# Full node ids in the buckets, tiles that run over their end, and all four marks of a step on VectorE, in a graph kernel on one core

## The reference, cut to what matters

```python
# x (6250,128); src, edge node ids (206250,); edge_attr_128 (206250,128); src is not sorted
edge_aggr = jnp.zeros((n, 128)).at[src].add(edge_attr_128)       # a sum of feature rows per node
combined  = concatenate([x, edge_aggr, global_feat repeated], -1) @ W_c + b_c
h = softplus(combined @ W1 + b1)
h = softplus(h @ W2 + b2)
out = layernorm(x + h @ W3 + b3)
```

## Time and profile before

| | |
|---|---|
| median of 3 runs | 2171.48 us (2169.77 to 2183.89) |
| the profiled execution | 2166.25 us |
| its span in the trace | 2164.6 us |
| PE busy | 1999.3 us (92%) |
| DVE, POOL, ACT busy | 1534.2, 1163.2, 843.7 us |
| placement, first to last `rank` | 72.4 to 1623.4 us |
| summing, first tile load to first MLP matmul | 1642.2 to 2082.8 us |

### The profile page before, as it was taken

The page is one execution under the profiler, slowest core; times in us unless marked ns, Lnnn a source line. Parts: engine busy times, 40 slices in busy tenths (PEclk is TensorE's granted clock), DMA queues, the critical chain, the costliest instruction groups (busy, mean ns, idle before and its releaser), DMA issues.

```text
span 2164.6 us, 62457 instructions
## 1 busy us (share of the span) xinstructions
PE 1999.3 (92%) x15732; PEld 1762.3 (81%) x15732; DVE 1534.2 (71%) x5104; ACT 843.7 (39%) x2517; POOL 1163.2 (54%) x1351
## 2 busy tenths in 40 slices
PE   6408999999999999999999999999996999999975
PEld 3307888888888888888888888888886999999952
DVE  7505776777677777777776777777775888888857
ACT  0002222222222222222222222222224888888877
POOL 2205665665665566656655556565564555455424
PEclk9658999999999999999999999999997999999998
DMA  9975665666656566566665565665556999999932
GB/s 353 150 140 153 173 175 167 174 178 170 178 171 176 173 170 180 168 177 171 173 178 164 168 183 168 170 181 173 176 153 222 296 285 284 284 284 283 284 98 55
DMA packets 345473, 414.30 MB, mean 191 GB/s; under 512 B 28261, under 2 KB 249465, under 8 KB 344273
## 3 DMA queue, kind: packets, MB, share of 16 engines
q1 hardware_dynamic: 284579, 247.08, 39.4%
q0 software_dynamic: 53184, 163.38, 26.1%
q10 hardware_dynamic: 7689, 3.60, 0.8%
HBM read 233.69 MB, written 180.24 MB: 191 GB/s over the span
## 4 chain that ended last, share of the span: by engine, by line
PE 69%; POOLq 6%; issue 6%; POOL 6%; another core or an unknown queue 4%; ACT 3%; ACTq 2%; DMA 1%; DVE 1%; SPq 0%; DVEq 0%
PE ps L953 55%; PE ps L961 5%; POOL sums L454 5%; POOLq L449 4%; PE ps L1019 3%; PE ps L938 3%; PE ps L932 2%; ACTq L759 2%; PE ps L936 1%; POOLq L453 1%; ACT arena L827 1%; DMA buckets<-arena,index 1%; ACT arena L830 1%; ACT arena L828 1%
## 5 line engine op out<-in xcount | busy, mean ns | idle before, releaser
L953 PE MATMUL ps<-arena 128*120 128x129 f32 x9672 | 1286.8, 282 | 73.2 <-ACT arena L784 73.1
L429 POOL DMA_INDIRECT buckets<-arena,index x806 | 893.1, 1108 | 664.6 <-ACT arena L784 300.6
L953 PEld LDWEIGHTS ps<-arena 128*120 128x120 f32 x9672 | 1128.4, 184 | 99.1 <-issue 73.2
L784 ACT ACTIVATE arena<-ps 120x387 f32<-120x387 f32 x806 | 397.8, 494 | 1146.5 <-PE ps L953 734.2
L614 DVE TENSOR_SCALAR arena<-slot_no,slot_f 128x360 f32<-128x360 f16 x1612 | 586.2, 404 | 0.0
L1019 PE MATMUL ps<-mark,members 128*128 128x128 f32 x3648 | 426.3, 279 | 19.8 <-ACT mark L859 19.8
L1019 PEld LDWEIGHTS ps<-mark,members 128*128 128x128 f32 x3648 | 418.7, 193 | 27.3 <-issue 20.0
L682 DVE TENSOR_SCALAR mark<-node_no,members 128x128 f32<-128x128 f16 x1368 | 365.0, 328 | 71.8 <-DMA members<-buckets 46.1
L601 DVE TENSOR_TENSOR picked<-hotc,ps 128x392 f32<-128x392 f16 x202 | 113.5, 562 | 348.2 <-PE ps L938 344.0
L454 POOL TENSOR_TENSOR sums<-sums,staged 128x128 f32 x456 | 216.0, 474 | 227.0 <-ACT staged L847 206.3
L620 DVE TENSOR_SCALAR reach<-block_no,arena 50x120 bf16<-50x120 f16 x806 | 196.8, 244 | 0.0
(11 more groups left out here) (121 smaller groups left out, 578.8 us busy)
## 6 DMA issues: line engine op xcount, KB each, us to landing
members<-buckets SPq DMA_DIRECT2D x456, 258.0 KB, 3.4
arena<-in_feats SPq DMA_DIRECT2D x201, 512.0 KB
buckets<-arena,index POOLq DMA_INDIRECT x806
buckets<-sums SPq DMA_DIRECT2D x4, 3096.0 KB, 26.4
arena<-in_xT SPq DMA_DIRECT2D x12, 250.0 KB, 5.8
xn<-in_x ACTq DMA_DIRECT2D x1, 2800.0 KB
out_rows<-xn SPq DMA_DIRECT2D x12, 224.0 KB
buckets<-sums SPq DMA_DIRECT2D x1, 1032.0 KB, 39.1
```

The source lines that it names most:

```text
L429: pool.indirect_dma_start(units, bass.IndirectOffsetOnAxis(ap=index[0:SLOTS, s, b:b + 1], axis=0), rows[0:SLOTS, b, :], None).then_inc(sca ...
L784: act.activation(rows[0:SLOTS, b, :], ps[0:SLOTS, MOVED + b, 0:BLK], ACT.Copy).then_inc(rows_ready, 1)
L953: mm = pe.matmul(ps[0:SLOTS, MOVED + b, r * ROWF:(r + 1) * ROWF], perm[0:TP, b, t, r * SLOTS:(r + 1) * SLOTS], feat[0:TP, s, b * TPB + t, ...
```

## The change

- The rows in the scratch carry their full node id plus one (`local1` is made in one operation from `ids_i`), no longer the id within the bucket.
- Buckets follow each other without alignment. A tile starts at any row, and its last rows may belong to the next bucket: their ids match none of the tile's 128 nodes. So the 11 pieces behind each bucket and the 52 zero tiles go; four small gap writes and one tile of zeros stay. The number of steps stays 456.
- A table `tile_row` holds each tile's first row. SP reads it into a register before each load (`value_load`) and then waits for `summed`.
- A mark compares `node_no + first_node` with the row's id: one DVE operation with two scalars read per partition, one of them at a place that the step number gives. DVE makes all four; ACT's L853 and L859 go.
- `window`, `first_node` and `past` are evicted by ACT behind its set-up work, before its first `set_locals`; DVE makes `tile_row` after the first body of `place`.
- `reach`, `goto3`, `boff1_16` and `ident16` are used over all 128 partitions (the added ones hold zeros), so the matmuls of `goto` and the last four of `rank` contract over 128 rows.

A step has one more mark and one more register operation. The diff, cut to its core:

```diff
-    SURE = -(-(E + K * STREAMS * GAP) // TROWS)
-    ZTILES = 12
+    ENDROW = E + K * STREAMS * GAP
...
@@ sync
-            for t in range(SURE, STEPS, ZTILES):
-                n = min(ZTILES, STEPS - t)
-                sp.dma_start(buckets[t * TROWS:(t + n) * TROWS, :].rearrange("(p r) f -> p (r f)", p=P),
-                             zero_src[:, 0:n * QR * ROWF]).then_inc(spare_zeroed, 16)
+            sp.dma_start(buckets[ENDROW:ENDROW + TROWS, :].rearrange("(p r) f -> p (r f)", p=P), zero_src[:, :])\
+              .then_inc(spare_zeroed, 16)
...
             def load_members(s, m):
+                row = sp.value_load(tile_row[0:1, bass.ds(s, 1)], min_val=0, max_val=ENDROW)
+                if not isinstance(s, int):
+                    sp.wait_ge(summed, s + (1 - MS))
                 sp.dma_start(members[:, m, :],
-                             buckets[bass.ds(s * TROWS, TROWS), :].rearrange("(p r) f -> p (r f)", r=QR))\
+                             buckets[bass.ds(row, TROWS), :].rearrange("(p r) f -> p (r f)", r=QR))\
                   .then_inc(members_loaded[m], 16)
@@ gpsimd
-            pool.wait_ge(spare_zeroed, 16 * -(-(STEPS - SURE) // ZTILES))
-            pool.wait_ge(zero_at_made, 2)
-            for z in range(ZEROS + STREAMS - 1):
-                n = (ZROWS if z < ZEROS else GAP) * ROWF
+            pool.wait_ge(zero_at_made, 1)
+            for o in range(STREAMS):
                 pool.indirect_dma_start(
-                    units, bass.IndirectOffsetOnAxis(ap=zero_at[0:K, z:z + 1], axis=0),
-                    zero_src[0:K, 0:n], None).then_inc(zeroed, 16)
+                    units, bass.IndirectOffsetOnAxis(ap=zero_at[0:K, o:o + 1], axis=0),
+                    zero_src[0:K, 0:GAP * ROWF], None).then_inc(zeroed, 16)
@@ vector
-            dve.tensor_scalar(local1[0:TP, :], key16[0:TP, :], float(-P), 1.0, ALU.mult, ALU.add).then_inc(local_a, 1)
-            dve.wait_ge(local_a, 1)
-            dve.tensor_tensor(local1[0:TP, :], local1[0:TP, :], ids_i[0:TP, :], ALU.add).then_inc(local_a, 1)
+            dve.tensor_scalar(local1[0:TP, :], ids_i[0:TP, :], 1.0, None, ALU.add).then_inc(local_a, 1)
...
-            dve.tensor_scalar(window[:, :], ps[0:1, WINDOW, 0:STEPS], -1.0, float(P), ALU.add, ALU.mult)\
-               .then_inc(window_made, 1)
+            def tile_rows():
+
+                dve.wait_ge(past_copied, 1)
+                dve.scalar_tensor_tensor(past[0:1, :], tile_no[0:1, :], float(TROWS), past[0:1, :], ALU.mult, ALU.add)\
+                   .then_inc(tile_row_a, 1)
+                dve.wait_ge(tile_row_a, 1)
+                dve.tensor_scalar(tile_row[:, :], past[0:1, :], float(ENDROW), None, ALU.min).then_inc(tile_row_made, 1)
...
-                dve.tensor_scalar(reach[0:KS, b, 0:SLOTS], block_no[0:KS, 0:SLOTS], border[0:KS, bass.ds(g, 1)], None,
-                                  ALU.is_ge)\
+                dve.tensor_scalar(reach[:, b, 0:SLOTS], block_no[:, 0:SLOTS], border[:, bass.ds(g, 1)], None, ALU.is_ge)\
                    .then_inc(reach_made, 1)
...
-                for r in range(QR - 1):
-                    last = dve.tensor_scalar(mark[:, m % 4, r, :], node_no[:, :],
-                                             members[:, m, r * ROWF + D:(r + 1) * ROWF], None, ALU.is_equal)
+                for r in range(QR):
+                    last = dve.tensor_scalar(mark[:, m % 4, r, :], node_no[:, :], first_node[:, bass.ds(s, 1)],
+                                             members[:, m, r * ROWF + D:(r + 1) * ROWF], ALU.add, ALU.is_equal)
                 last.then_inc(marked, 1)
@@ scalar
+            act.wait_ge(window_done, 2)
+            act.activation(window[:, :], ps[0:1, WINDOW, 0:STEPS], ACT.Copy, scale=float(P)).then_inc(window_made, 1)
+            act.activation(first_node[:, :], ps[:, WINDOW, 0:STEPS], ACT.Copy, scale=float(P)).then_inc(window_made, 1)
+            act.activation(past[0:1, :], ps[0:1, PAST, 0:STEPS], ACT.Copy).then_inc(past_copied, 1)
...
-            def last_apart(s, m, turn):
...
-            def last_mark(s, m):
...
@@ tensor
-                    mm = pe.matmul(out_[:, b, :, :], boff1_16[0:K, bass.ds(c * CB + b, 1)].to_broadcast([K, TP]),
-                                   ident16[0:K, 0:K].unsqueeze(1).to_broadcast([K, TPB, K]), start=False,
+                    mm = pe.matmul(out_[:, b, :, :], boff1_16[:, bass.ds(c * CB + b, 1)].to_broadcast([P, TP]),
+                                   ident16[:, 0:K].unsqueeze(1).to_broadcast([P, TPB, K]), start=False,
                                    stop=(b == nb - 1))
...
-                pe.matmul(ps[0:SLOTS, GOTO + s % 2, b * 3:(b + 1) * 3], reach[0:KS, b, 0:SLOTS],
-                          goto3[0:KS, bass.ds(g, 1), :].rearrange("p g j -> p (g j)"), start=True, stop=True)\
+                pe.matmul(ps[0:SLOTS, GOTO + s % 2, b * 3:(b + 1) * 3], reach[:, b, 0:SLOTS],
+                          goto3[:, bass.ds(g, 1), :].rearrange("p g j -> p (g j)"), start=True, stop=True)\
                   .then_inc(reach_used, 1)
...
             def sum_members(s, m):
                 pe.wait_ge(marked, s + 1)
-                pe.wait_ge(last_marked, s + 1)
```

More of the change, by code:

```diff
@@ L137, in gnn_bucketed_edge_sum_mlp_layernorm @@
         small16 = sb("small16", [P, 1], f16)
-        zero_at = sb("zero_at", [P, ZEROS + STREAMS - 1], i32)
+        zero_at = sb("zero_at", [P, STREAMS], i32)
         window = sb("window", [1, STEPS], i32)
+        tile_row = sb("tile_row", [1, STEPS], i32)
+        first_node = sb("first_node", [P, STEPS])
         slot_f = sb("slot_f", [P, 2, CB * TPB])
@@ L150, in gnn_bucketed_edge_sum_mlp_layernorm @@
         staged = sb("staged", [P, 4, P])
-        apart = sb("apart", [P, 2, P])
         wc = sb("wc", [P, 3, D])
@@ L227, in gnn_bucketed_edge_sum_mlp_layernorm @@
         goto_a = sem("goto_a")
-        starts_made = sem("starts_made")
+        ends_made = sem("ends_made")
+        past_copied = sem("past_copied")
+        tile_row_a = sem("tile_row_a")
+        tile_row_made = sem("tile_row_made")
         window_done = sem("window_done")
@@ L540, in _ @@
                .then_inc(tiles_a, 1)
+            dve.tensor_copy(small[0:KS, 0:1], incl_f[0:KS, JB - 1:JB]).then_inc(tiles_made, 1)
             dve.wait_ge(tiles_a, 1)
@@ L565, in _ @@
                                      ALU.mult, ALU.add).then_inc(places_made, 1)
+            dve.wait_ge(iota_set, 6)
             dve.wait_ge(base_a, 1)
-            dve.tensor_scalar(starts16[0:KS, :], tile_no[0:KS, :], small[0:KS, 0:1], None, ALU.is_ge)\
-               .then_inc(starts_made, 1)
+            dve.tensor_scalar(ends16[0:K, :], tile_no[0:K, :], small[0:K, 4:5], None, ALU.is_ge).then_inc(ends_made, 1)
             for h in range(2):
@@ L664, in _ @@
             place_body(0)
+            tile_rows()
             with dve.Fori(1, BODIES) as i:
@@ L847, in evict_sums @@
                 act.activation(staged[:, m % 4, :], ps[:, m, 0:P], ACT.Copy).then_inc(evicted, 1)
-            def last_apart(s, m, turn):
-                act.wait_ge(members_loaded[m], turn * 16 + 16)
-                wait(act, last_marked, s - 1)
-                act.activation(apart[:, m % 2, :], node_no[:, :], ACT.Abs, scale=-1.0,
-                               bias=members[:, m, QR * ROWF - 1:QR * ROWF]).then_inc(apart_made, 1)
-            def last_mark(s, m):
-                act.wait_ge(apart_made, s + 1)
-                wait(act, summed, s - 3)
-                act.activation(mark[:, m % 4, QR - 1, :], apart[:, m % 2, :], ACT.Relu, scale=-1.0, bias=1.0)\
-                   .then_inc(last_marked, 1)
-            def act_step(s, m, turn):
-                ends = isinstance(s, int)
-                if not ends or s + 3 < STEPS:
-                    last_apart(s + 3, (m + 3) % MS, turn + (m + 3) // MS)
-                if not ends or s + 2 < STEPS:
-                    last_mark(s + 2, (m + 2) % MS)
-                evict_sums(s, m)
-            last_apart(0, 0, 0)
-            last_mark(0, 0)
-            last_apart(1, 1, 0)
-            last_mark(1, 1)
-            last_apart(2, 2, 0)
             for m in range(MS):
-                act_step(m, m, 0)
-            with act.Fori(1, STEPS // MS - 1) as i:
+                evict_sums(m, m)
+            with act.Fori(1, STEPS // MS) as i:
                 for m in range(MS):
-                    act_step(i * MS + m, m, i)
-            for m in range(MS):
-                act_step(STEPS - MS + m, m, STEPS // MS - 1)
+                    evict_sums(i * MS + m, m)
             for step in range(NCH + 4):
@@ L907, in _ @@
             pe.wait_ge(tables16_set, 3)
-            pe.wait_ge(ones_set, 5)
+            pe.wait_ge(ones_set, 7)
             pe.wait_ge(whole_made, 1)
@@ L912, in _ @@
                   .then_inc(boff_done, 1)
-            pe.wait_ge(tiles_made, 1)
-            pe.matmul(ps[0:KS, SMALL, 0:1], tri16[0:KS, 0:KS], small16[0:KS, 0:1], start=True, stop=True)\
```

(11 more changed lines are left out.)

60 lines of the change are left out of this document (28 added, 32 removed).

## The result

| | kernel before | kernel changed |
|---|---|---|
| median, first comparison | 2171.50 us (2169.77 to 2183.89, 4 runs) | 2207.71 us (2196.84 to 2220.85, 4 runs) |
| ratio | | 1.0157, 95% interval 1.0089 to 1.0225 |
| profiled execution; span | 2166.25; 2164.6 us | 2204.69; 2202.9 us |

A forecast was written before the change was run, and what follows sets the result against it. PE was taken to bound placement; in summing SP would become the bound. From 2166.25 us: set-up -4.5, stall -77, placement -212, summing +161 gave 2033.8, with half the way to the median 2036 us; range 1950 to 2175.

The forecast's parts named there:

- Placement, -212 us: Placement stage: the chunk of four batches falls from 7.33 to 6.25 us over 201 chunks, less 5 us for slow starts.
- The rows' part: Placement matmuls: 128 rows throughout hide weight loads, so a batch falls from 1.66 to 1.42 us, `rank` 0.64 to 0.49.
- Rival A: Placement: number formats expose weight loads too, so only `rank` gains; chunk 7.15 us, 2216 us, slower by 2%; chance 0.12.
- Set-up and stall: Before and early in placement: set-up -4.5 us without the zero writes' traffic, and PE's 73.14 us stall gone, -77 us.
- Rival E: Early placement: the stall moves, as the first scatter waits for x and features; at most 20 us return, 2056 us; chance 0.05.
- Summing: Summing stage: SP's register load and address work make SP the bound, step 0.93 to 1.29 us, +161 us.
- rival C: Summing: SP's register load is slow, standing behind the DMA issue; 1.62 us a step, +148 us, 2184 us; chance 0.13.
- the marks are hidden: Summing: DVE's four marks a step, 0.88 to 1.08 us, hide under SP's 1.29 us and add no time.
- 1.08 us at the most: Summing: upper bound for DVE's four marks a step, from 0.81 us for three now; lower bound 0.88 us.
- Rival D: Summing: SP's load is hidden and DVE binds at 1.0 us a step; 130 us less, 1906 us; chance 0.08.
- Rival B: Placement: the scatter ring binds, ACT waiting for landings; chunk 7.0 us, 150 us more, 2186 us; chance 0.10.
- slower: Outcome for the whole kernel: slower than before, by rival A or by B with C together; chance 0.13.

The follow-up runs named there:

- e8: The changed kernel, unedited, in another session: 2036.06 us, ratio 0.9442 to the kernel before.
- e1: Changed kernel with VectorE's wait for `goto` moved from the end of a chunk to behind the next chunk's first batch: 2204.53 us, ratio 1.0140.
- e3: Kernel before with nothing but the 128-row operands of `reach`, `goto` and `rank`: 2145.44 us, ratio 0.9863.
- e12: The kernel of e4 (TensorE waits for its own signal) run again, in a session with late signals: 2205.97 us, ratio 1.0153.
- e5: Changed kernel with SyncE's tile loads at fixed rows, without the register load: 1989.78 us.
- e7: Changed kernel with both edits: tile loads without the register load, and marks with one scalar: 1901.90 us.
- e6: Changed kernel with marks that compare with one scalar and add no first node: 2032.08 us.
- e11: The kernel before, unedited, with a second trace: 2163.35 us, beside seven runs with a median of 2172.22 us.
- e4: Changed kernel with one more wait: before batch g TensorE waits for its own signal of batch g - 2: 2040.99 us, ratio 0.9472.
- e17: Changed kernel with GpSimd's placement scatters replaced by plain writes that ScalarE issues to consecutive rows: 2009.13 or 2004.00 us, by listing order 2004.00 us.
- e18: The changed kernel, unedited, beside e17: 2041.87 us, ratio 0.9471.
- e2: Changed kernel with the 50- and 49-row operands of `reach`, `goto` and the last part of `rank` put back: 2238.75 us, ratio 1.0293.

## Why the prediction was wrong, point by point

- **The failed step** is "Placement, -212 us": "I take 6.25, near the lower end, as ACT's waits stop PE nowhere in this stretch". In the first comparison the chunk is 7.15 us. The step took for granted that the others see a matmul's end when it ends. They saw it about 0.9 us later on the mean, up to 4.2 us (VectorE's starts), and with a batch of 1.43 instead of 1.66 us that stopped the ring of engines. The same program shows it from both sides, in the first comparison and in e8; and wherever the signals were late, a kernel with 128 rows had a chunk of 7.06 to 7.17 us (first comparison, e1, e3, e12), and wherever they were prompt and the scatters stood, of 6.28 to 6.37. The traces of the cause itself are the two timelines, VectorE's starts and, as far as they are complete, the semaphores' records. No run moved the lateness alone, and what makes it was not found.
- **The rows' part was right.** Batch 1.43 us against 1.42, `rank` 0.43 against 0.49. In e8 the chunk is 6.33 against 6.25. The Trainium skill, TensorEngine Tiling (Array Packing), Key Properties, says that a change of the tiling mode drains the engine. The trace agrees as far as it goes, though no row names the mode: with equal rows the matmul behind L943 starts 1005.73 - 1005.70 = 0.03 us after it, where it was 0.15 in the kernel before. Rival A is refuted. That e8 meets the 2036 us to 0.1 us is luck: its first to last `rank` takes 1273.2 us against a forecast of 1261.7, its summing 594.6 against 601.7, and these two misses mostly cancel. The yardstick beside it was 2155 and not 2171 us, so that the gain was 119 us where 135 were forecast.
- **Set-up and stall were right:** -3.6 against -4.5, and 77 against 77 us of stall. Rival E did not come.
- **Summing was right in its sum, but not in its parts:** +154.7 against +161. SyncE's step is 1.27 us against 1.29, and its register load takes 268 ns at the median (the row below), so rival C is refuted. The Trainium skill, DMA: Bandwidth & Descriptors, Latency and other measured facts, puts the floor of such a load at about 600 ns; the traces don't agree, with 268 ns on SyncE and 287 on GpSimd. That the marks are hidden held, but "1.08 us at the most" was wrong: they take 1.189 us a step (e5). The bounds came from marks with one scalar, and a second one costs more: in e5 a mark fills VectorE for 100 / 337 = 0.297 us, in e7 with one scalar for 100 / 404 = 0.248 at the most (TensorE is full there too). The error was covered by the 0.09 us that SyncE's step is longer. Rival D is refuted with it: e6 freed VectorE and the step stayed, and e5 took the register load away and it fell.
- **Rival B** (7.0 us, 2186) has nearly the chunk and the time of the first comparison, but not the mechanism: ScalarE's waits for landings fell from 159.5 us in 1300 to 88.9 us in the whole placement, as far as the incomplete records tell, and where the chunk was 6.33 they rose to 626 us in 1000 without stopping TensorE.
- **Chances.** The range ended at 2175 and gave 0.13 to "slower", nearly all of it to A, which is refuted. No case was held for "the engine's work shrinks, but its signals don't come sooner", though the trace of the kernel before shows 35% of the ranks late (16% in e11, its second trace).
- **A slip without effect:** 0.88 of 1.29 us is 68%, which is less than the 74% that it is called "no less than". The clock was granted in full all the same (1.00 at 1800 to 1900 us, where TensorE was busy for 90.5%).

Line L356 of the changed kernel, 1800 to 1900 us (ns min/median/max):

```profile
L356 SPq TENSOR_LOAD <-tile_row x79: 263/268/278, 1800.3 to 1899.0; - x79
```

## What to carry to other kernels

Before an engine's gaps are counted as gain, measure in the trace of before how long after its last matmul the waiting engine starts, over many cases and not by the median alone; a lateness that a slower engine hides becomes the bound of the faster one. Run a surprising result again beside its yardstick in another session before explaining it: one edit (e4) seemed to give 167 us, and gave none. Count whether each signal has its record before reading waits from a trace. Where a bound is relieved, know the second one: in the summing the next stood 7% lower, and only both edits together paid.

## What the runs showed of the hardware

- The same program took 2207.71, 2036.06 and 2041.87 us in three sessions, and the kernel before 2171 or 2155, and the chip numbered 0 (e1 to e3; e17 and e18) gave both. In the engines' own work I found no difference: the median durations of ScalarE's, VectorE's and GpSimd's instructions agree within 1 ns (L791 493, L616 402, L432 997 in the first). Late are TensorE's signals alone: where GpSimd waited for ScalarE's eviction, it started 0.83 us behind its end at the median in both the first trace and e8, and TensorE's `goto` started 0.14 us behind the `reach` it had waited for in the first. Missing, though, are records of all three of VectorE, ScalarE and TensorE, and of the DMAs' landings (15977 in the first, 24143 in e8).
- With late signals TensorE goes on for some time, and now and then stops in the middle of a batch, with nothing to wait for that the trace shows, until they are let out:

```profile
1075.30 1.32 PE L935 MATMUL ps<-arena 128*120 128x129 f32 x8
1077.69 0.61 PE L935 MATMUL ps<-arena 128*120 128x129 f32 x4 [1.06 <-issue]
```

  At 1077.71 a signal of `move` is written, the first since 1071.72, though batches ended at 1072.42 and 1073.85, and four more of TensorE's follow within 0.27 us.
- In late sessions VectorE started 0.57 to 1.08 us on the mean after a rank's end where all matmuls of the stage had 128 rows (the changed kernel, e1, e3, e12), and 0.16 to 0.33 where some had 49 and 50 (the kernel before, e2, e11).
